# Cross attention of a two-layer fp32 model: order of the score copies, turned maxima, early loads and the last unit

## The reference, cut to what matters

```
q = (query @ Wq + bq).reshape(B, L, NKV, G, HDIM)      # B=8, L=64, NKV=8, G=4, HDIM=128
k_, v_ = jnp.split(kv @ Wkv + bkv, 2, axis=-1)         # kv: 8 x 1601 x 512
k = k_.reshape(B, Lk, NKV, HDIM)
v = v_.reshape(B, Lk, NKV, HDIM)
scores = jnp.einsum('blkgd,bmkd->bkglm', q, k) * scale
attn = jax.nn.softmax(scores, axis=-1)
o = jnp.einsum('bkglm,bmkd->blkgd', attn, v).reshape(B, L, NHEAD * HDIM)
return o @ Wo + bo
```

## Time and profile before

| what | value |
|---|---|
| median of 3 runs | 3044.93 us (3043.64 to 3046.32) |
| the profiled execution | 3044.76 us, span 3042.9 us |
| cross attention, first key tile to last output | 119.5 to 2076.0 us of the span |
| busy over the span: PE / DVE / ACT / POOL | 88% / 67% / 48% / 49% |
| mean granted TensorE clock | 0.95 of full speed |

### The profile page before, as it was taken

One profiled execution on the slowest core, in us unless ns is written; L12 is line 12 of the kernel. 1 busy time (PEld: TensorE's weight loads), 2 busy tenths in 40 slices (PEclk: granted clock), 3 DMA queues, 4 the chain that ended last, 5 costly groups with the idle time before them and its releaser, 6 DMA issues. The chain is left out here.

```text
span 3042.9 us, 47641 instructions
## 1 busy us (share of the span) xinstructions
PE 2681.1 (88%) x17160; PEld 2406.8 (79%) x17160; DVE 2026.7 (67%) x2299; ACT 1446.0 (48%) x2582; POOL 1477.8 (49%) x961
## 2 busy tenths in 40 slices
PE   8899999999999999999999999996875667996878
PEld 6799999989999999999989999995751225774666
DVE  2266766776677666776676677664459997776783
ACT  3355555555445545554555555553345442442542
POOL 2344734644554463464473464421009971685652
PEclk9999999999999999999999999997977998997879
DMA  5310110110111011011111010004231002432100
GB/s 207 107 44 23 56 44 29 47 54 22 34 43 53 24 49 51 28 43 51 35 43 46 27 57 22 29 5 173 92 110 56 1 14 90 144 136 73 46 1 14
DMA packets 92429, 168.98 MB, mean 56 GB/s; under 512 B 8451, under 2 KB 57859, under 8 KB 89147
## 3 DMA queue, kind: packets, MB, share of 16 engines
q1 hardware_dynamic: 81610, 153.75, 15.2%
q10 hardware_dynamic: 10608, 12.32, 1.2%
HBM read 146.05 MB, written 19.73 MB: 54 GB/s over the span
## 5 line engine op out<-in xcount | busy, mean ns | idle before, releaser
L299 POOL TENSOR_TENSOR xa_pt_lo<-xa_st,xa_pt_hi 128x1024 fp32r<-128x1024 f32 (+1 forms) x256 | 522.4, 2069 | 756.8 <-ACT xa_pt_hi L466 756.8
L54 PE MATMUL xa_kv_ps<-xa_wv_hi,ctx_hi 128*128 128x256 f32 (+1 forms) x1664 | 480.2, 289 | 14.8 <-DVE xa_v_lo L545 13.1
L56 PE MATMUL xa_kv_ps<-xa_wv_hi,ctx_lo 128*128 128x256 f32 (+1 forms) x1664 | 469.2, 282 | 0.0
L55 PE MATMUL xa_kv_ps<-xa_wv_lo,ctx_hi 128*128 128x256 f32 (+1 forms) x1664 | 465.6, 280 | 0.0
L54 PE MATMUL xa_kv_ps<-ctx_hi,xa_wk_hi 128*128 128x402 f32 (+1 forms) x1024 | 363.5, 355 | 14.3 <-POOL xa_wk_lo L262 10.9
L56 PE MATMUL xa_kv_ps<-ctx_hi,xa_wk_lo 128*128 128x402 f32 (+1 forms) x1024 | 354.0, 346 | 0.0
L55 PE MATMUL xa_kv_ps<-ctx_lo,xa_wk_hi 128*128 128x402 f32 (+1 forms) x1024 | 354.0, 346 | 0.0
L461 ACT ACTIVATE xa_st<-xa_st 128x1024 f32<-128x1024 f32 (+1 forms) x256 | 227.6, 902 | 226.0 <-DVE xa_st L575 221.8
L54 PEld LDWEIGHTS xa_kv_ps<-xa_wv_hi,ctx_hi 128*128 128x128 f32 (+1 forms) x1664 | 306.4, 184 | 27.2 <-DVE xa_v_lo L545 21.1
L545 DVE TENSOR_TENSOR xa_v_lo<-xa_kv_ps,xa_v_hi 128x512 fp32r<-128x512 f32 (+1 forms) x224 | 145.6, 650 | 255.9 <-ACT xa_v_hi L439 255.9
L55 PEld LDWEIGHTS xa_kv_ps<-xa_wv_lo,ctx_hi 128*128 128x128 f32 (+1 forms) x1664 | 308.2, 185 | 0.8
(11 more groups left out here) (368 smaller groups left out, 7047.4 us busy)
## 6 DMA issues: line engine op xcount, KB each, us to landing
ca_nat<-in_ctx SPq DMA_DIRECT2D x48, 512.0 KB, 4.9
ctx_raw<-in_ctx_t SPq DMA_DIRECT2D x24, 804.0 KB, 6.5
xa_wk_raw<-in_xa_wk SPq DMA_DIRECT2D x64, 256.0 KB, 2.7
xa_wv_raw<-in_xa_wv SPq DMA_DIRECT2D x32, 512.0 KB, 4.5
q_raw<-in_xa_wq SPq DMA_DIRECT2D x8, 1024.0 KB, 4.9
q_scratch<-q_q_sb ACTq DMA_DIRECT2D x8, 1024.0 KB, 4.4
xa_q_raw<-q_scratch SPq DMA_DIRECT2D x64, 128.0 KB, 2.5
o_scratch<-xa_o_sb SPq DMA_DIRECT2D x64, 128.0 KB, 1.7
```

The source lines that it names most:

```text
L54: nc.tensor.matmul(out, left[0], right[0], start=first, stop=False)
L55: nc.tensor.matmul(out, left[0], right[1], start=False, stop=False)
L56: return nc.tensor.matmul(out, left[1], right[0], start=False, stop=last)
L299: nc.gpsimd.tensor_tensor(by_chunk(pt_lo, p), scored(j, p).rearrange("p g q c -> p g c q"), by_chunk(pt_hi, p).bitcast(F32), ALU.subtract) ...
```

## The change

Seven things change.

1. ACT, odd unit: the pieces 0 and 1 of `high` leave the unit, and key tiles 2 and 3 are drained one step earlier. All four pieces of `high` are now copied in the even unit that follows, one behind the first three score copies, one behind the last, and two between the key tiles. (This is done for even units alone.)
2. PE, even unit: `turn_maxima` stands behind three key tiles of the next unit, not two. ACT and DVE drain the key tiles before they go on with the diagonal and the shifts.
3. DVE, odd unit: key tile 2 is read ahead of the last shift, key tile 3 right behind it, and both sums come after.
4. The weights `wk` of heads 0 and 1 and `wv` of head pair 0 are loaded and split in the stage of the queries (`EarlyWeights`), and ACT no longer waits there for the last store of `q`. SP waits for it in the next stage, ahead of the loads of `q`.
5. `ready`, which POOL sets after two memsets, is waited for behind the first four key tiles and not ahead of them, and POOL sets it after splitting two heads of `q`.
6. The last unit goes in finer steps: ACT makes an exponential and its high part in turn, DVE writes the first piece of `pt_lo`, the denominators are made behind the second piece of `attend`, into `m_ps`, and their reciprocal is taken while PE finishes.
7. The first inputs of `attention_output` are loaded in unit 6 of the last batch, into the space of the raw context and of `wv_raw` (`OutputInputs`). Its later loads alternate between that space and one buffer of its own.

```diff
+class EarlyWeights:
...
+    def load(self, sp):
+        sp.dma_start(self.wk_raw[:, 0], self.wk[0]).then_inc(self.wk_in[0], 16)
+        sp.dma_start(self.wv_raw[:, :, :], self.wv[0]).then_inc(self.wv_in, 16)
+        sp.dma_start(self.wk_raw[:, 1], self.wk[1]).then_inc(self.wk_in[1], 16)
...
+class OutputInputs:
...
+    def load(self, sp, j):
+        sp.dma_start(self.o_raw, self.o_dram[:, j].rearrange("b d n -> d b n")).then_inc(self.arrived, 16)
+        for h in range(2):
+            sp.dma_start(self.w_raw[h], self.wo[j][:, 2 * h:2 * h + 2]).then_inc(self.arrived, 16)
...
             def first():
+                for i in range(2):
+                    pool.wait_ge(q_in[i], 16)
+                    halves(q_hi[:, i], q_lo[:, i], q_raw[:, i], 4 + i).then_inc(q_split, 1)
                 nc.gpsimd.memset(ones_r[:, :].bitcast(F32), 1.0)
                 nc.gpsimd.memset(st[:, :, NG - 1, :, :], 0.0).then_inc(ready, 1)
-                key_weights(0, 0, True)
-                value_weights(0, 0, True)
-                key_weights(0, 1, True)
...
-                    for _ in range(2):
+                    for _ in range(3):
                         key_tile(b, j + 1, keys.pop(0))
                     turn_maxima(b, j)
...
             def group(b, j, last, alone=False):
-                copies(b, j)
                 if j % 2 == 0:
+                    copies(b, j, 0, 3)
+                    if not alone:
+                        high(b, j - 1, 0)
+                    copies(b, j, 3, NG)
+                    if not alone:
+                        high(b, j - 1, 1)
+                    key_tile(b, j + 1, 0)
                     if not alone:
                         high(b, j - 1, 2)
+                    key_tile(b, j + 1, 1)
+                    if not alone:
                         high(b, j - 1, 3)
-                    key_tile(b, j + 1, 0)
-                    key_tile(b, j + 1, 1)
+                    key_tile(b, j + 1, 2)
                     diagonal(b, j)
-                    exponential(b, j, 0)
-                    key_tile(b, j + 1, 2)
-                    exponential(b, j, 1)
                     key_tile(b, j + 1, 3)
-                    exponential(b, j, 2)
-                    exponential(b, j, 3)
+                    for p in range(NP):
+                        exponential(b, j, p)
...
+                elif has_keys(j, last):
+                    copies(b, j, 0, NG)
                     diagonal(b, j)
...
+                    key_tile(b, j + 1, 1)
                     exponential(b, j, 1)
+                    key_tile(b, j + 1, 2)
                     exponential(b, j, 2)
...
                     exponential(b, j, 3)
-                    high(b, j, 0)
...
-                    high(b, j, 1)
...
+                else:
+                    copies(b, j, 0, NG)
+                    diagonal(b, j)
+                    for p in range(NP):
+                        exponential(b, j, p)
+                        high(b, j, p)
+                        if p == 0:
+                            with_bias(b, j - 1)
...
-            for i in range(2):
-                act.wait_ge(q_out[i], (NKV // 2 + 1) * 16)
```

More of the change, by code:

```diff
@@ L105, in cross_attention @@
+def cross_attention(nc, context, early, following, wk, wv, bk, bv, ident, ones, q_dram, o_dram):
     B, _, KC, S = context.ctx_t.shape
@@ L242, in group @@
                         context.load(sp, b + 1, t)
+                if j == NKV - 2 and last:
+                    sp.wait_ge(o_out[0], (b * (NKV // 2) + j // 2 + 1) * 16)
+                    sp.wait_ge(ctx_lo_set, B * NT)
+                    sp.wait_ge(wv_split, B * NKV // 2)
+                    following.load(sp, 0)
             def first():
-                weights(0, 0, True)
                 sp.dma_start(bk_sb[:, :], bk).then_inc(bias_in, 16)
                 sp.dma_start(bv_sb[:, :], bv).then_inc(bias_in, 16)
-                weights(0, 1, True)
+                for i in range(2):
+                    sp.wait_ge(early.q_out[i], (NKV // 2 + 1) * 16)
+                for i in range(2):
+                    sp.dma_start(q_raw[:, i], q_dram[0, i]).then_inc(q_in[i], 16)
                 weights(0, 2)
@@ L294, in split_ctx, with low @@
                     nc.gpsimd.tensor_tensor(lo, raw, hi.bitcast(F32), ALU.subtract).then_inc(ctx_lo_set, 1)
-            def low(b, j):
-                for p in range(NP):
+            def low(b, j, start=0):
+                for p in range(start, NP):
                     pool.wait_ge(hi_set, unit(b, j) * NP + p + 1)
@@ L312, in group @@
                     key_weights(b, j + 2)
-                low(b, j)
+                low(b, j, 1 if last and j == NKV - 1 else 0)
                 if j == NKV - 2 and not last:
@@ L379, in spread_maxima, with denominators, attend @@
                 nc.tensor.matmul(m_ps[:, 1, :], ones_r[:, :], diag[:, :], start=True, stop=True).then_inc(bm_full, 1)
-            def attend(b, j, between=None):
+            def denominators(b, j, alone=False):
+                pe.wait_ge(sum_set, unit(b, j) + 1)
+                return nc.tensor.matmul(d_ps(j, alone), ones[:, :], sums[:, 2, :], start=True, stop=True)
+            def attend(b, j, between=None, alone=False):
                 pe.wait_ge(on_set, unit(b, j) + 1)
@@ L441, in value_tile, with copies @@
                                      ACT.Copy).then_inc(kv_hi, 1)
-            def copies(b, j):
-                for g in range(NG):
+            def copies(b, j, start, until):
+                for g in range(start, until):
                     m = min(2, NC - 2 * g)
@@ L739, in split_on_pool, with queries @@
     return nc.gpsimd.tensor_tensor(lo, src, hi.bitcast(F32), ALU.subtract)
-def queries(nc, x_sb, ident, xt_hi, xt_lo, wq, bq, q_dram, context):
+def queries(nc, x_sb, ident, xt_hi, xt_lo, wq, bq, q_dram, context, early):
     NKV, _, KC, GD = wq.shape
@@ L757, in queries @@
         q_full, q_set = sc.sem("q_full"), sc.sem("q_set")
-        q_out = [sc.sem(f"q_out{i}") for i in range(2)]
+        q_out = early.q_out
         def load(sp):
@@ L775, in _ @@
             context.split_first(pool)
+            early.split(pool)
         @block.sync
@@ L787, in _ @@
                 context.load(sp, 0, t)
+            early.load(sp)
         def evacuate(act, j0, i):
@@ L861, in attention_output @@
         bias_in = sc.sem("bias_in")
-        a_in = [sc.sem(f"a_in{i}") for i in range(2)]
+        a_in, IN = [early.arrived, sc.sem("a_in1")], (48, 32)
         hi_set, lo_set, used, done, x_set = (sc.sem(n) for n in ("hi_set", "lo_set", "used", "done", "x_set"))
```

212 lines of the change are left out of this document (127 added, 85 removed).

## The result

The changed kernel takes 3105.03 us (median of 4 runs, 3103.75 to 3107.15) against 3044.88 before: ratio 1.0199, 95% interval 1.0183 to 1.0214. It is 60 us slower than before, where 3042.5 was forecast, and it lies outside the forecast's range. The profiled run has a span of 3102.8 us.

A forecast was written before the change was run, and what follows sets the result against it. It took TensorE as the bound, busy 227.49 of 240 us. From 3044.76: -10.6 -2 +26.4 -5.6 -0.7 -9.8 = -2.3, so 3042.5 us; own case 3034 to 3051, 8 in 10 range 3018 to 3063.

The forecast's parts named there:

- Even unit, up to the third key tile: Joins held behind POOL's `low` delay `k_lo`; PE's third key tile starts at +13.65 us, where it was +11.98.
- Even unit, from there on: Third key tile to next unit: 28.95 us before, +0.2 for two transposes, -1.0 for `v_lo` waits, so 28.15.
- the term of +26.4: Even units: each takes 41.8 us, +0.85 (0.6 to 1.1), times 31, range +19 to +34.
- The one on the slower side: Rival: POOL catches the maxima in the seven context units, +20 us, 3062; chance 0.18.
- the two faster cases: Rivals in even units: joins not caught, 2982 us, chance 0.08; only one caught, 3022 us, chance 0.10.
- The seams as a whole: Stage start and end give 23 us; a rival had them give less, 3048 us, chance 0.12.
- Odd units: Sums move behind the key tiles, where DVE has room; PE hides it, so no change.
- Context units: Seven odd units that split the next batch's context: L564 ends earlier, 0.8 us gained each, -5.6 in all.
- Ahead: Seam before the stage: first scores at 120.4 us, where they began at 131.07, -10.6 (-8 to -11).
- unit 0: First unit: its longest wait for `v_lo`, 2.7 us, mostly goes, -2 (0 to -3).
- last unit: End of the stage: a denominator is gained ahead, but `low` on DVE makes `with_bias` late, -0.7 us (+2 to -3).
- outputs: Seam behind the stage: first high part of the outputs at 2079.3 us, where it was 2089.13, -9.8 (-6 to -10).

The follow-up runs named there:

- e5: The changed kernel with the two joins of the maxima replaced by reductions of one input: 3024.55 us, against 3043.41 for the kernel before.
- e6: The changed kernel with 21 matmuls nobody reads between the second and third key tile of even units: 3052.85 us, against 3043.41 for the kernel before.
- e3: The changed kernel with the maxima turned behind two key tiles again, on TensorE alone: 3153.27 us, against 3047.30 for the kernel before.
- e1: The changed kernel with the steady units of before put back, only changes 4 to 7 kept: 3024.10 us, against 3047.30 for the kernel before.

## Why the prediction was wrong, step by step

**Even unit, up to the third key tile: right.** Forecast +13.65, measured +13.48, with the joins held as worked out (L560 to +12.2, measured +12.0; the last one to +13.0, measured +12.9). That the cause is the second SBUF input is shown by e5, where a join with one input ran through a `low`, and by `v_lo`, which is of the join's operation with one SBUF input and was never held. The Trainium skill, "SBUF — State Buffer", section on who interferes with whom, says the same of the shared port pair, and that a reduction does not contend. The runs agree: the reduction takes 0.70 beside a `low` (e5).

**Even unit, from there on: the step that failed.** The prediction took 28.95 us of before, at full clock, and subtracted the small waits: 28.15. Measured: 29.91 (13.48 to 43.39) in unit 4. With the clock held up, in e6, it is 28.36, so the rest of this step was right. The prediction had worked out itself that "PE stands 3 to 4 us here for `k_lo`" and did not ask what the clock does behind such a wait. Ten to eleven matmuls at 0.336 in place of 0.183 are the missing 1.7 us; in some units it is 2.9. In total the term of +26.4 was +87: 31 with the clock held up (e6), and 56 for the clock, a cost that the prediction put at nothing without a reason.

The trace of before had no wait of this length in its steady units: its longest for L564 was 1.2, at a clock of 1.00. But it had the warning. The longest wait for `v_lo`, 2.7 in unit 0, is followed by a stretch at half the clock:

```profile
155.79 0.39 PE L54 MATMUL xa_kv_ps<-xa_wv_hi,ctx_hi 128*128 128x256 f32 x1 [2.69 <-DVE xa_v_lo L545]
...
156.30:159.60 3.30, 3.30 (x17) 3.30 (x17) 2.95 (x3) 0.55 (x2) 3.30 (x2) 0.50 0.00 0
```

Half of 3.3 us is 1.65 us of work. An estimate from this row for 31 waits of 3 to 4 us is 51 us more, 3094 in place of 3042.5.

The Trainium skill, "TensorE: Matmul & The Clock Gate", section on HAM oscillation, describes a kernel in which a wait stands ahead of each tile and each tile then starts at the low clock. The even units of the changed kernel agree (0.54 behind the wait in unit 4). The prediction did not weigh this page.

**The rivals.** None of the four named this. The one on the slower side (GpSimd catching the maxima of the context units) did not come: the third `ctx_lo` ended at +7.13 and the first join began at +6.93, 0.2 us from the point where it decides (0.1 to 0.4 in the seven units). In e3, with the same order of ACT, DVE and POOL, it came in three of the seven. The joins were caught, both of them, so the two faster cases were wrong. The seams as a whole gave what they should.

**Odd and context units, seams: right.** Odd units unchanged (18.91). Context units -1.0 each, -6.9 in all (forecast -5.6). Ahead -10.1 (-10.6), unit 0 -2.05 (-2), last unit -0.8 (-0.7), outputs -8.8 (-9.8). e1 has the seams without the rest: -23.2 by the medians (forecast -23.1), though unit 0 gave nothing there. The -2 of unit 0 was luck: the wait for `v_lo` that was to go is still there in the changed kernel, 3.10 us long, and what went with the new order are the waits for `k_lo` (1.49 and 0.20).

**The chances.** The range was made from errors of single terms of known kinds. The forecast of a new wait of 4 us, over three times longer than any for `k_lo` or the maxima in the steady units of before, ought to have widened the range on the slower side alone.

Open: why the clock falls behind a wait of 2.43 us in 14 of 24 units and not in the other 10, and what makes the low stretch in some units longer. No run was made for this.
